# The gram directly behind the prediction on TensorE, in a delta-rule attention kernel

## The chip, the cores and the metric

One core of one Trainium2 chip. The metric is device time in microseconds of one launch; the median of several runs is given. Engines are named as in the profile: PE is TensorE (PEld its weight loads), DVE VectorE, ACT ScalarE, POOL GpSimd, SP the queue that issues all DMAs here.

## The reference

The input x has the shape (B=4, T=4096, D=512), with H=16 heads of width 32. The block is a delta-rule attention between two layer norms, then a feed-forward product with ternary weights between two more. Cut to the attention:

```python
rk = x.reshape(B, T, H, 32); rk = rk / max(norm(rk), 1e-12)      # x is the layer-normed input
wk = pad(rk[:, :-1], one step of zeros in front)                 # write key = previous read key
v, gate, beta = x @ Wv.T, sigmoid(x @ Wg.T), sigmoid(x @ Wb.T)
for t in range(T):                                               # per batch and head, S is 32x32
    pred = wk_t @ S
    S    = S + outer(wk_t, (v_t - pred) * beta_t)
    o_t  = (rk_t @ S) * gate_t
out = o @ Wo.T;  x = x + layernorm(out);  x = x + layernorm(ffn(layernorm(x)))
```

## The kernel before

The program has three stages one after the other: a setup of the weights (`setup`), the attention (`attention`) and the feed-forward product (`feed_forward`). Only PE's program in `attention` is changed.

**Tiling.** Time is cut into 128 tiles of C=32 time steps; a tile has the 4 batches x 32 steps on the 128 partitions. Within a tile the recurrence is solved in closed form: a triangular system (1 + M) e = v − pred per batch and head, with M from the gram of the keys. DVE inverts these systems by elimination, two tiles at a time, so its work in odd and in even steps of the loop differs: the matrices are turned in (L752) at the start of an even step and turned out (L816) at the end of an odd one.

**Software pipeline.** Each engine has a function `step(base, j)` that is written out for j from -13 to 134. In one step it works on many tiles at once, each shifted by a lag (`LAG_...`): tile j itself is in the chain of the state, tile j+6 (`LAG_GRAM`) has its gram made, tile j+7 (`LAG_V`) its values, keys and gates, tile j+9 (`LAG_TURN`) its x turned, tile j-3 (`LAG_Y`) its output product. An engine does its instructions in just the order in which `step` writes them; the engines meet by semaphores that count. That hand-written order is what sets the order of the work around the change.

**PE's step before** (`step`, L933 on). The names of its parts:

- `predict` (L949, 16 products on 32-column tiles of the array, 32 passes in the profile): `ps_chain` = state x `key_bd`, the block-diagonal write keys of tile j. ACT copies it to `rhs` (L611, semaphore `turned_done`).
- `turn_back` (L956, 4 transposes) turns `rhs` back into `ps_chain`; DVE then makes `rhs` = `val` − `ps_chain` (L831, semaphores `pred_psum` and `rhs_done`).
- `value(first, end)` (L925, `ps_v<-wv,xt`): some of the 12 products that make the values of tile j+7.
- gram (L981): `ps_gram` = `kt` x `kbd` for tile j+6, 16 products on 32-column tiles, copied by ACT (L674, `gram_done`) and masked by POOL (L571).
- `solve_error(half)` (L962, 32 small products): applies the inverse to `rhs`. Its wait is `error_ready`: `tt_done` and `rhs_done`.

Then x is turned (L1003, needs ACT's copy of gram, because both use the bank `ps_gram`), the keys are turned (L1011, needs ACT's copy of the values, L681, because both use `ps_v`), the output product `ps_y` and the state update (L1024) take turns, o is turned (L1048), and the gates are made (L925, `ps_v<-wgb,xt`).

**The keys for the gram.** `kbd` is block-diagonal and is filled by DMA: ACT copies the turned keys to `kt` (L702), SP waits for that copy and issues four DMAs (L456), and PE's `gram_ready` waits for them with `kbd_loaded`, in the next step:

```python
wait(pe, s["ot_done"], upto(j - 1 + LAG_OUT + 1))
wait(pe, s["xt_done"], upto(times(base, BODY, j + LAG_TURN)))
wait(pe, kbd_loaded[l % 2], halves(base, j, LAG_GRAM) * (16 * HB) + 16 * HB)
```

**SP's step** issues, in this order, the load of x (L430), two small copies of the gate (L436, L440), four DMAs of `key_bd` (L448), four of `kbd` (L456), the residual x (L461) and the store of x1 (L465).

Of the kernel before, what the change touches and what calls it, by code (L numbers as in the profile page):

```python
# [272 lines left out]
def attention(nc, io, k):  # L273
    with ExitStack() as ctx:
# [6 lines left out]
        def sem(name):  # L281
            return ctx.enter_context(nc.semaphore(name))
# [79 lines left out]
        s = {n: sem(n) for n in names}  # L362
# [7 lines left out]
        def on(base, step, lag):  # L370


            n = times(base, BODY, step + lag)
            return n, (step + lag) % BODY, not isinstance(n, int) or 0 <= n < NT

        def upto(count):
            return min(count, NT) if isinstance(count, int) else count
# [5 lines left out]
        def wait(eng, semaphore, count):  # L383

            if not isinstance(count, int) or count > 0:
                eng.wait_ge(semaphore, count)
# [497 lines left out]
        def _(pe):  # L884
# [14 lines left out]
            def error_ready(base, j):  # L899

                n, l, live = on(base, j, 0)
                if live:
                    wait(pe, s["tt_done"], times(base, BODY // 2, j // 2 + 1))
                    wait(pe, s["rhs_done"], n + 1)

            def gram_ready(base, j):

                n, l, live = on(base, j, LAG_GRAM)
                if live:
# [3 lines that stand above are left out]
# [8 lines left out]
            def project(out, lhs, weights, steps):  # L921

                for i in steps:
                    kb, (a, w) = i // 3, PARTS3[i % 3]
                    last = pe.matmul(out, lhs[:, a, kb, :], weights[:, w, kb, :], start=(i == 0), stop=(i == 3 * KB - 1))  # L925
                return last
# [4 lines left out]
            SHARE = WHOLE // 4  # L931

            def step(base, j):  # L933

                n, l, live = on(base, j, 0)
                v, v_l, v_live = on(base, j, LAG_V)
                m, m_l, m_live = on(base, j, LAG_GRAM)

                def value(first, end):
                    if v_live:  # L940
                        return project(ps_v[:, :], xt[:, v_l % 4], k["wv"], range(first, end))

                def predict():
                    if live:
                        for g in range(KB):
                            for i in range(HB):
                                h = HB * g + i
                                out = ps_chain[HD * i:HD * i + HD, P * g:P * g + P]
                                last = pe.matmul(out, state[:, l % 2, HD * h:HD * h + HD], key_bd[:, :, h, :], start=True, stop=True)  # L949
                        last.then_inc(s["turned_psum"], 1)  # L950

                def turn_back():
                    if live:
                        wait(pe, s["turned_done"], n + 1)
                        for g in range(KB):
                            last = pe.transpose(ps_chain[:, P * g:P * g + P], rhs[:, P * g:P * g + P], k["ident"][:, :])  # L956
                        last.then_inc(s["pred_psum"], 1)
# [7 lines left out]
                if live and not on(base, j - 1, LAG_Y)[2]:  # L965
                    chain_ready(base, j)
                predict()
                if v_live:
                    wait(pe, s["gexp_done"], v)
                    wait(pe, s["xt_done"], upto(v + 2))  # L970
                value(0, SHARE + 1)
                turn_back()
                value(SHARE + 1, SHARE + 2)
                gram_ready(base, j)
                value(SHARE + 2, SHARE + 3)
                if m_live:
                    for g in range(KB):
                        for b in range(B):
# [1 line left out]
                            out = ps_gram[q, :].rearrange("p (i h) -> p h i", h=H)[:, HB * g:HB * g + HB, :]  # L980
                            last = pe.matmul(out, kt[:, m_l % 2, g, q], kbd[:, m_l % 2, :, g, q], start=True, stop=True)  # L981
                    last.then_inc(s["gram_psum"], 1)
                value(SHARE + 3, 3 * SHARE - 1)
                error_ready(base, j)
                value(3 * SHARE - 1, 3 * SHARE)
                solve_error(0)
# [73 lines left out]
                if y_live:  # L1060
                    last.then_inc(s["y_psum"], 1)
            run(step)


# [293 lines left out]
```

## Time and profile before

| | us |
|---|---|
| median of 3 runs | 2329.17 |
| lowest and highest run | 2324.87, 2331.81 |
| profiled execution, span of its first to last instruction | 2313.7 |
| profiled execution, own time | not given by the page |
| PE busy | 2084.1 (90%) |
| DVE busy | 1992.1 (86%) |
| ACT busy | 1774.0 (77%) |
| POOL busy | 1729.0 (75%) |

A busy time is the sum of an engine's instructions, counted from the first start to the last end, and matmuls that overlap count once. The span does not hold what lies before the first and behind the last instruction. The attention stage runs to about 1950 us, the feed-forward stage from there to the end. A wait "PE ps_v L925 <- DMA kbd<-kt" reads: PE stood idle ahead of an instruction of line 925 that writes `ps_v`, until the DMA that writes `kbd` from `kt` had landed. Where the gram's wait stands ahead of a value product, as before the change, it is that product which shows it.

### The profile page before, as it was taken

Reading aid. Unit: us, or ns where it says so; the run is one execution under the profiler, and the core shown is the slowest. Engines: PE = TensorE matmul, PEld = TensorE weight load, DVE = VectorE, ACT = ScalarE, POOL = GpSimd, SP = SyncE. Lnnn points to the kernel's source line nnn. Section 1 sums busy time; section 2 is a strip of 40 time slices with the busy share of each in tenths; the row PEclk is TensorE's granted clock in tenths of the full one; section 3 lists DMA queues with packets and bytes.
Section 4 is the critical chain, followed back from the end, with each engine's and each line's share of the span. In section 5 each row is a group of like instructions: output and inputs, shape, how many; then the busy total and the mean of one; then the engine's idle time right before and its main releaser. Section 6 shows DMA issues by size and latency. Waiting matters only on the chain. (4 is left out here: it accounts for less than half of the span.)

```text
span 2313.7 us, 123730 instructions
## 1 busy us (share of the span) xinstructions
PE 2084.1 (90%) x50216; PEld 1316.0 (57%) x50216; DVE 1992.1 (86%) x5810; ACT 1774.0 (77%) x3756; POOL 1729.0 (75%) x3099
## 2 busy tenths in 40 slices
PE   1679999999999999999999999999999987499997
PEld 1346666666666666666655656566666654255554
DVE  5388999999999999999889999899999994588886
ACT  3667888888888888888877878788888744477775
POOL 2668888888888888888888888888888854244443
PEclk7789999999999999999999999999999988799999
DMA  2122333333333333333333333333333222488885
GB/s 86 48 65 80 98 100 98 98 98 95 99 97 99 94 94 95 95 94 94 93 91 93 94 96 91 94 97 96 100 96 99 82 78 67 150 225 229 225 231 129
DMA packets 156632, 247.69 MB, mean 107 GB/s; under 512 B 39544, under 2 KB 39552, under 8 KB 156064
## 3 DMA queue, kind: packets, MB, share of 16 engines
q1 hardware_dynamic: 156064, 239.78, 36.6%
q8 instruction: 397, 6.50, 1.2%
q14 instruction: 171, 1.40, 0.2%
HBM read 104.40 MB, written 67.11 MB: 74 GB/s over the span
## 5 line engine op out<-in xcount | busy, mean ns | idle before, releaser
L800 DVE TENSOR_TENSOR ps_elim<-ps_elim,sys 128x30 f32<-128x30 f32 (+14 forms) x1920 | 543.3, 326 | 0.7
L808 DVE TENSOR_TENSOR sys<-sys,ps_elim 128x30 f32<-128x30 f32 (+14 forms) x1920 | 534.6, 316 | 1.0
L925 PE MATMUL ps_v<-wv,xt 128*128 128x512 f16 x1536 | 435.2, 389 | 39.6 <-DVE rhs L831 16.5
L925 PE MATMUL ps_y<-wo,ot 128*128 128x512 f16 x1536 | 406.1, 386 | 17.3 <-DVE x L852 9.5
L962 PEld LDWEIGHTS ps_chain<-rhs,t_t 32*32 32x32 f32 x16384 | 257.3, 144 | 110.6 <-issue 110.5
L962 PE MATMUL ps_chain<-rhs,t_t 32*32 32x32 f32 x16384 | 286.1, 218 | 13.9 <-issue 8.5
L709 ACT ACTIVATE state<-ps_s 128x512 f32<-128x512 f32 x128 | 76.5, 598 | 265.6 <-PE ps_s L1024 263.6
L1024 PEld LDWEIGHTS ps_s<-err,key_b 32*32 32x32 f32 x16384 | 172.1, 106 | 147.4 <-issue 147.2
L1310 PE MATMUL ps_f<-wq,f_xq 128*128 128x512 f16 x1024 | 242.5, 381 | 6.8 <-DVE f_xq L1276 6.8
L538 POOL TENSOR_TENSOR x_part<-x_hat,x_part 128x512 f16<-128x512 f32 x128 | 148.7, 1162 | 131.6 <-ACT x_hat L645 111.5
L1024 PE MATMUL ps_s<-err,key_b 32*32 32x32 f32 x16384 | 205.5, 195 | 34.2 <-issue 34.2
L925 PEld LDWEIGHTS ps_v<-wv,xt 128*128 128x128 f16 x1536 | 121.0, 99 | 188.4 <-issue 120.5
L925 PEld LDWEIGHTS ps_y<-wo,ot 128*128 128x128 f16 x1536 | 130.2, 98 | 130.3 <-issue 26.3
L831 DVE TENSOR_TENSOR rhs<-val,ps_chain 128x512 f32<-128x512 f32 x128 | 87.4, 682 | 121.1 <-PE ps_chain L956 121.1
L1158 POOL TENSOR_TENSOR f_y_veps<-f_y_var,y_eps 128x1 f32<-128x1 f32 x128 | 53.6, 418 | 184.3 <-ACT f_unread L1191 183.4
L585 POOL TENSOR_TENSOR pred<-val,err 128x512 f32<-128x512 f32 x128 | 163.1, 1274 | 11.3 <-ACT err L688 11.2
L571 POOL TENSOR_TENSOR m_t<-gram,b_mask 128x512 f32<-128x512 f32 x128 | 163.5, 1277 | 5.3 <-ACT gram L674 5.2
L512 POOL TENSOR_TENSOR b_mask<-gates,neg_mask 128x512 f32<-128x512 f32 x128 | 135.5, 1059 | 32.0 <-DVE gates L879 31.9
L1310 PEld LDWEIGHTS ps_f<-wq,f_xq 128*128 128x128 f16 x1024 | 100.2, 98 | 102.0 <-DVE f_xq L1276 7.5
L577 POOL TENSOR_TENSOR o_part<-o_g,o_part 128x512 f16<-128x512 f32 x128 | 148.5, 1160 | 0.0
L949 PE MATMUL ps_chain<-key_bd,state 128*32 128x128 f32 x4096 | 139.9, 277 | 4.3 <-issue 2.8
L714 ACT ACTIVATE ot<-ps_gram 128x1024 f16<-128x1024 f16 x128 | 130.9, 1022 | 16.8 <-PE ps_gram L1048 16.7
(163 smaller groups left out, 5123.6 us busy)
## 6 DMA issues: line engine op xcount, KB each, us to landing
x_in<-in_L_attn_x SPq DMA_DIRECT2D x128, 256.0 KB
kbd<-kt SPq DMA_DIRECT2D x512, 64.0 KB, 2.1
key_bd<-key_t SPq DMA_DIRECT2D x512, 64.0 KB, 2.4
x_res<-in_L_attn_x SPq DMA_DIRECT2D x128, 256.0 KB
x_scratch<-x SPq DMA_DIRECT2D x128, 256.0 KB, 6.3
f_x<-x_scratch SPq DMA_DIRECT2D x32, 1024.0 KB, 7.6
out<-f_res SPq DMA_DIRECT2D x128, 256.0 KB, 3.9
gate<-gates SPq DMA_DIRECT2D x128, 7.9 KB
```

The source lines that it names most:

```text
L512: pool.tensor_tensor(b_mask[:, :, :], beta.unsqueeze(1).to_broadcast([P, C, H]), k["neg_mask"][:, :].unsqueeze(2).to_broadcast([P, C, H]), ...
L538: pool.tensor_tensor(x_part[:, l % 2, 1, :], x_hat[:, l % 4, :], x_part[:, l % 2, 0, :], ALU.subtract).then_inc(s["xlo_done"], 1)
L571: pool.tensor_tensor(m_t[:, :, l % 2, :], gram[:, :, :], b_mask[:, :, :], ALU.mult).then_inc(s["mt_done"], 1)
L577: pool.tensor_tensor(o_part[:, l % 2, 1, :], o_g[:, :], o_part[:, l % 2, 0, :], ALU.subtract).then_inc(s["olo_done"], 1)
L585: pool.tensor_tensor(pred[:, :], val[:, l, :], err[:, l % 2, :], ALU.subtract).then_inc(s["pred_done"], 1)
L800: dve.tensor_tensor(tmp, factors(r, c, first, end)[:, c - first:C - 1 - first, c - first:c - first + 1].to_broadcast(shape), sys[:, r, c:c ...
L808: dve.tensor_tensor(dst, dst, tmp, ALU.add).then_inc(elim_done[r], 1)
L925: last = pe.matmul(out, lhs[:, a, kb, :], weights[:, w, kb, :], start=(i == 0), stop=(i == 3 * KB - 1))
L949: last = pe.matmul(out, state[:, l % 2, HD * h:HD * h + HD], key_bd[:, :, h, :], start=True, stop=True)
L962: last = pe.matmul(ps_chain[q, e], t_t[q, l // 2 % 2, :, l % 2, h], rhs[q, e], start=True, stop=True)
L1024: last = pe.matmul(ps_s[q, e], key_b[q, l, e], err[q, l % 2, e], start=(isinstance(n, int) and n == 0 and h == 0), stop=True, skip_group_c ...
L1310: last = pe.matmul(ps_f[i][:, :], xq[:, r % 2, a, kb, P * i:P * i + P], k["wq"][:, kb, :], start=(m == 0), stop=(m == 2 * KB - 1))
```

## The change

In PE's step the gram and its `gram_ready` are moved directly behind `predict`. `turn_back` follows the gram, and the value products that stood between and around these groups (four ahead of `turn_back`, two behind it, and those behind the gram) now stand in one row behind `turn_back`, up to the one behind `error_ready`. The waits of the first value product (`gexp_done`, `xt_done`) move with it. No instruction is added or removed, and the other engines' programs are the same.

```diff
@@ -965,14 +965,7 @@
                 if live and not on(base, j - 1, LAG_Y)[2]:
                     chain_ready(base, j)
                 predict()
-                if v_live:
-                    wait(pe, s["gexp_done"], v)
-                    wait(pe, s["xt_done"], upto(v + 2))
-                value(0, SHARE + 1)
-                turn_back()
-                value(SHARE + 1, SHARE + 2)
                 gram_ready(base, j)
-                value(SHARE + 2, SHARE + 3)
                 if m_live:
                     for g in range(KB):
                         for b in range(B):
@@ -980,7 +973,11 @@
                             out = ps_gram[q, :].rearrange("p (i h) -> p h i", h=H)[:, HB * g:HB * g + HB, :]
                             last = pe.matmul(out, kt[:, m_l % 2, g, q], kbd[:, m_l % 2, :, g, q], start=True, stop=True)
                     last.then_inc(s["gram_psum"], 1)
-                value(SHARE + 3, 3 * SHARE - 1)
+                turn_back()
+                if v_live:
+                    wait(pe, s["gexp_done"], v)
+                    wait(pe, s["xt_done"], upto(v + 2))
+                value(0, 3 * SHARE - 1)
                 error_ready(base, j)
                 value(3 * SHARE - 1, 3 * SHARE)
                 solve_error(0)
```

On PE, in a step of the full pipeline, before (the names are those of the parts above; `ps_v<-wv,xt` is a value product, `ps_chain<-ident,rhs` the turn back):

```order
L949 MATMUL ps_chain<-key_bd,state 32x128 x16
L925 MATMUL ps_v<-wv,xt 128x512 x4
L956 MATMUL ps_chain<-ident,rhs 128x128 x4
L925 MATMUL ps_v<-wv,xt 128x512 x2
L981 MATMUL ps_gram<-kbd,kt 32x4x32 x16
L925 MATMUL ps_v<-wv,xt 128x512 x3
L962 MATMUL ps_chain<-rhs,t_t 32x32 x32
```

and now, at the same place:

```order
L949 MATMUL ps_chain<-key_bd,state 32x128 x16
L974 MATMUL ps_gram<-kbd,kt 32x4x32 x16
L956 MATMUL ps_chain<-ident,rhs 128x128 x4
L925 MATMUL ps_v<-wv,xt 128x512 x9
L962 MATMUL ps_chain<-rhs,t_t 32x32 x32
```

The gram has moved ahead of the turn back and of six value products; its line is now L974.

On PE, in a step ahead of the chain (tiles whose gram is made before tile 0 enters it), with the waits, before:

```order
L925 MATMUL ps_v<-wgb,xt 128x32 [waits kt_done]
L925 MATMUL ps_v<-wgb,xt 128x32 x11
L925 MATMUL ps_v<-wv,xt 128x512 [waits xt_done,gexp_done]
L925 MATMUL ps_v<-wv,xt 128x512 x4
L925 MATMUL ps_v<-wv,xt 128x512 [waits kbd_loaded0,xt_done]
L981 MATMUL ps_gram<-kbd,kt 32x4x32 x16
L925 MATMUL ps_v<-wv,xt 128x512 x6
```

and now:

```order
L925 MATMUL ps_v<-wgb,xt 128x32 [waits kt_done]
L925 MATMUL ps_v<-wgb,xt 128x32 x11
L974 MATMUL ps_gram<-kbd,kt 32x4x32 [waits kbd_loaded0,xt_done]
L974 MATMUL ps_gram<-kbd,kt 32x4x32 x15
L925 MATMUL ps_v<-wv,xt 128x512 [waits xt_done,gexp_done]
L925 MATMUL ps_v<-wv,xt 128x512 x11
```

The wait for `kbd_loaded` stood behind five value products and now stands ahead of all twelve.

## Rows read from the trace of the kernel before

**Rows 1.** Busy time by stretch: stretch, its length, each engine's busy us, clock, DMA
```profile
727.00:1299.00 572.00, 537.46 (x14823) 347.02 (x14821) 517.98 (x1660) 465.21 (x1016) 485.27 (x859) 1.00 0.33 94
1299.00:1815.00 516.00, 494.36 (x13682) 319.37 (x13680) 475.46 (x1531) 431.21 (x935) 449.13 (x794) 1.00 0.33 95
```

**Rows 2.** Waits, whole span: who waited for whom, us in total, times, longest
```profile
DVE rhs L831 <- PE ps_chain L956: 121.1, 67, 8.5
...
PE ps_v L925 <- DVE rhs L831: 16.5, 31, 1.4
...
PE ps_v L925 <- DMA kbd<-kt: 15.5, 15, 2.2
```

**Rows 3.** Timeline of PE, a middle step: start us, us, line, operation
```profile
1004.24 1.08 PE L949 MATMUL ps_chain<-key_bd,state 128*32 128x128 f32 x32
1005.25 1.04 PE L925 MATMUL ps_v<-wv,xt 128*128 128x512 f16 x4
1006.16 0.66 PE L956 MATMUL ps_chain<-ident,rhs 128*128 128x128 f32 x4
1006.65 0.59 PE L925 MATMUL ps_v<-wv,xt 128*128 128x512 f16 x2
1007.17 1.08 PE L981 MATMUL ps_gram<-kbd,kt 128*32 128x128 f32 x32
1008.19 0.82 PE L925 MATMUL ps_v<-wv,xt 128*128 128x512 f16 x3
1008.94 1.11 PE L962 MATMUL ps_chain<-rhs,t_t 32*32 32x32 f32 x64
...
1011.78 0.62 PE L1003 MATMUL ps_gram<-ident_half,x_part 128*128 128x128 f16 x8
1012.28 0.63 PE L1011 MATMUL ps_v<-ident,key 128*128 128x128 f32 x4
```

**Rows 4.** Timeline of ACT, the same step
```profile
1002.19 0.60 ACT L709 ACTIVATE state<-ps_s 128x512 f32<-128x512 f32 x1 [2.65 <-PE ps_s L1024]
...
1011.07 0.58 ACT L674 ACTIVATE gram<-ps_gram 128x512 f32<-128x512 f32 x1
1011.55 0.59 ACT L681 ACTIVATE val<-ps_v 128x512 f32<-128x512 f32 x1
...
1013.52 0.62 ACT L702 ACTIVATE kt<-ps_v 128x512 f32<-128x512 f32 x1
```

**Rows 5.** Timeline of SP: the four issues of kbd for this step
```profile
999.57 2.54 SPq L456 DMA_DIRECT2D kbd<-kt  x4
```

**Rows 6.** The tile kbd, whole span
```profile
DMA to landing us min/median/max: 1.9/2.1/3.8
```

**Rows 7.** Waits from 60 to 193 us, and PE's timeline in one such step
```profile
PE ps_v L925 <- DMA kbd<-kt: 11.4, 6, 2.2
...
72.31 1.25 PE L925 MATMUL ps_v<-wv,xt 128*128 128x512 f16 x5 [0.38 <-ACT g_exp L720]
75.58 0.58 PE L925 MATMUL ps_v<-wv,xt 128*128 128x512 f16 x1 [2.02 <-DMA kbd<-kt]
```

**Rows 8.** Waits from 193 to 515 us, and PE's timeline in one held step
```profile
PE ps_v L925 <- DMA kbd<-kt: 4.1, 9, 1.0
...
303.18 1.08 PE L949 MATMUL ps_chain<-key_bd,state 128*32 128x128 f32 x32
...
306.28 0.38 PE L925 MATMUL ps_v<-wv,xt 128*128 128x512 f16 x1 [0.31 <-DMA kbd<-kt]
...
308.72 1.11 PE L962 MATMUL ps_chain<-rhs,t_t 32*32 32x32 f32 x64
```

**Rows 9.** Timelines of SP and PE, a late step
```profile
1600.63 3.33 SPq L456 DMA_DIRECT2D kbd<-kt  x4
...
1603.79 1.08 PE L949 MATMUL ps_chain<-key_bd,state 128*32 128x128 f32 x32
...
1607.70 7.18 SPq L448 DMA_DIRECT2D key_bd<-key_t  x4
```

## The prediction

> **What bounds the kernel now.** I read busy time by stretches first, then the waits, then the timelines of PE, ACT and SP for one step of the attention stage, then the waits again by stretches. The change lies in the attention stage (to about 1950 us). From 727 to 1299 us, 39 steps of 14.7 us, PE is busy for 537 of 572 us at the full granted clock of 1.00 (2.4 GHz); from 1299 to 1815, 36 steps of 14.3 us, for 494 of 516, DVE for 475 and POOL for 449 [rows 1]. Four queues fill a step nearly whole: PE, ACT, DVE and the DMA queue of SP. So a gain on PE counts only where none of the other three ends later.
>
> The waits show which of them does. DVE waits 121.1 us for the turned-back prediction, nearly all in odd steps, and PE waits 16.5 us for DVE's `rhs` in 31 steps and 15.5 us for the block-diagonal keys `kbd` in 15 [rows 2]. These two take turns with PE; they are no slack that adds up.
>
> One step in the middle, read from PE's timeline [rows 3]: predict at 1004.24, four value products, turn back at 1006.16, two value products, gram at 1007.17, three value products, solve at 1008.94. The turned x then starts at 1011.78 and the turned keys at 1012.28. ACT in the same step [rows 4]: it begins with `state` at 1002.19 after an idle of 2.65 us, and from there it works without a gap to the copy of gram (ends 1011.65) and of the values (ends 1012.14). PE's turned x needs the first and starts 0.13 us behind it; the turned keys need the second and start 0.14 us behind it. So in such a step PE is paced by ACT's queue from predict to the keys, though it looks busy all the way.
>
> The last thing to look at is when `kbd` lands, since the gram waits for it. SP issues its four DMAs in a row after `kt` is copied. The last of the four issues of the middle step starts about 0.6 us before the row ends, at 1001.5 [rows 5], and landing takes 2.1 us in the median, 3.8 at most [rows 6]: landed at 1003.6, that is 0.6 us before predict starts.
>
> **The change, part by part.** No instruction is added or removed, on no engine. On PE the gram goes from behind the sixth value product to directly behind predict; SP's queue is as it was.
>
> (a) *Two changes of shape fall away.* The small-tile groups (predict, gram) now stand side by side. A further value product adds 0.22 us (groups of 4, 3 and 2 are 1.04, 0.82 and 0.59 long), but two of them ahead of the gram take 0.52 us and three ahead of the solve 0.75, so going over to small tiles costs about 0.09 us [rows 3]. Going back isn't shown by itself; I bound it by 0 and 0.2 (the gram's 1.02 us can't hold much more than that) and take 0.13, a little above the side that rows 3 show. With 0.04 us by which the transposes now wait for ACT behind four products, a step could save 0.26 us, over 118 steps 31 us. Of this I count nothing in the middle stretch: the turned x and keys still start when ACT's copies of gram and values end, and ACT's queue is not moved. Where DVE's `rhs` is last, it is nothing either, as DVE's own queue leads from one turn back to the next solve. It counts only as something to set against new waits.
>
> The Trainium skill, TensorEngine Tiling (Array Packing), Key Properties, says that changing the tiling mode drains TensorE; by that the order with fewer changes is the faster one, and it speaks for this change. The trace agrees: 0.09 us each time [rows 3].
>
> (b) *The gram is due 2.07 us earlier.* Before, it started 2.93 us after predict, and the product that carries its wait at about 2.6 us. Now it could start 0.9 us after predict (predict's 1.01 us less the tail that the change of shape cost). And the wait no longer has six value products in front: turn back, `rhs` on DVE and all nine products ahead of the solve are queued behind it. While `kbd` is out, PE has nothing to do. The transposes keep their time if it is landed: 0.9 + 1.02 is 1.92, what it was [rows 3].
>
> So per step the price is (landing − 0.8) where that is positive, less 0.26, less what DVE's lateness covered already. By stretches:
>
> *Start, 60 to 193 us.* In six steps without the chain PE does five products, waits for `kbd`, and does the sixth and the gram; these waits are 11.4 us in all [rows 7]. The loop kt, kbd, gram, values, keys, kt is serial there. The five products (1.25 us with their tail, five times 0.22 without) now come behind the landing: 6 x 1.08 = **6.5 us**. In three of the first four steps with the chain the keys land late as well, about 1 us each: **3 us**.
>
> *Early, 193 to 515 us, 23 steps.* PE waits for `kbd` in 9 [rows 8], although it is due only at 2.6 us. Predict starts at 303.18 and the held product at 306.28: landed near 306.2, 3.0 us after predict. Now the gram starts at 306.25, turn back 1.02 later at 307.27, then 0.49 for the transposes and 9 x 0.22 + 0.05 for the products: the solve starts at 309.8 instead of 308.72 [rows 8]. That is 1.1 us x 9 = 9.9; the other 14 land about 1 us after predict, 0.15 each, 2.1. Together **12 us**.
>
> *515 to 727 us, 15 steps.* No wait for `kbd` before. I find four steps where the four issues take as long as in rows 9 (landing about 2 us after predict), each 0.9: **3.5 us**.
>
> *Middle, 727 to 1299 us, 39 steps.* Landed before predict, as in rows 5, in nearly all of them: **0 us**.
>
> *Late, 1299 to 1815 us, 36 steps.* SP is behind. Its four issues begin at 1600.63 and last 3.33 us [rows 9], so the last starts at 1603.4 and lands at 1605.5, 1.7 us after predict (1603.79); most of the 36 are like this, 1.1 to 2.3. Before, this was early enough. Now the gram waits 0.85 us. In even steps DVE's `rhs` is late by as much and covers it. In the 18 odd ones 0.85 − 0.26 − 0.12 (the distance to ACT) = 0.45 us are left, 8 us, and up to 13 with spill into even steps. Against this, SP here issues on end (7.18 us for the four of `key_bd` just behind [rows 9]), without waiting for PE: PE held once by 0.85 us is closer to SP afterwards, and then pays only for fluctuations, 4 us. I take **6 us**.
>
> Sum: 6.5 + 3 + 12 + 3.5 + 0 + 6 = 31 us on the profiled span of 2313.7, so 2344.7. The runs' median of 2329.17 lies 15.5 us above this span (what is around it, and no time of that execution itself is given); the same 31 us on top give **2360 us**.
>
> If the cover goes: if DVE were earlier in even steps, the late stretch would pay there too; the next thing late behind a delayed turn back is `rhs`, then the value copy on ACT, then `kt`, which starts the next `kbd`. That loop is why the delay isn't made good.
>
> **The rivals.**
>
> *It gains (0.07).* If PE's own time, not ACT's, sets the step, the 0.26 us count. Against it: the 0.13 and 0.14 us by which PE follows ACT in rows 3 and 4 repeat in nearly every middle step. For it: PE's busy share. The rule of the Trainium skill's page TensorEngine Tiling points to this case too. The price: −31 us over 118 steps, +9.5 at the start, +7 early: 2315 us. It decides where ACT's copies end more than 0.12 us before PE gets there, and where `kbd` lands within 0.8 us of predict.
>
> *No difference (0.12).* If SP's queue is the real pace (each step's issues follow the last without a gap), then holding PE once brings it to SP's side, and all later waits are time that the step had to take anyway. Left are 6.5 at the start less some tenths per step in the middle: 2330 to 2336. For it: PE already waits for SP now and then. Against: in the early stretch SP begins again when `kt` is done, so a held PE holds SP.
>
> *It costs much more (0.15).* PE's small matmuls also stand idle for "issue" in the middle, where a step is 14.7 us against 14.3 in the late stretch [rows 1]. If the new phase between PE and the DMAs puts the late 36 steps into this state, that is 36 x 0.35 = 13 us, and with every landing of early and late steps unmoved relative to predict (5 + 7 more): 2329 + 31 + 25 = 2385 us, and more where both come on top of spill.
>
> **How the numbers follow.** Forecast 0.66, gain 0.07, no difference 0.12, much more 0.15. A measurement of this kernel tells about 0.3%, 7 us, from no change. The forecast and the costly case are both slower by more: 0.81. The no-difference case is taken as same, the gain as faster: 0.07. The forecast's own bounds: the early and late stretches at half (6 + 2), the start at 6.5 and a tenth gained in each of 40 middle steps (−4) give +10, 2340; the unmoved landings give 2372. To leave out no more than 2 in 10 the range goes from 2334 to 2386.
>
> **What would show it.** In the profile after: PE's timeline has 32 gram matmuls behind predict, then turn back, then nine value products. The wait for `kbd` now stands ahead of the gram, in some 50 to 60 steps instead of 15, with 40 to 60 us in total instead of 15.5, in the stretches named and hardly any from 727 to 1299. DVE's wait for the turned-back prediction grows in the same odd steps. In the middle the turned x and keys still start 0.13 us behind ACT's copies and the step keeps its 14.7 us. The solve starts about 4.4 us after predict where `kbd` is landed, 4.7 before. I am wrong if the middle steps get shorter (the gain), if few waits on `kbd` appear although PE gets no faster, or if the early stretch grows by less than 5 us.

## The result and the profile after

| | before | after |
|---|---|---|
| median | 2327.02 us (4 runs, 2323.01 to 2331.81) | 2376.68 us (4 runs, 2365.9 to 2385.66) |
| ratio, with its 95% interval | | 1.0215 [1.018, 1.025] |
| profiled execution: span | 2313.7 | 2364.2 |
| its own time | | 2365.9 |

The kernel is 49.7 us slower by the medians and 50.5 by the spans. The forecast was 2360, so the direction and the range held, and of the loss 31 us were foreseen. A second time, in a later group of runs, the changed kernel took 2350.92 against 2310.65, 1.018 [1.0159, 1.0201], 40.3 us more (a2 below).

Busy time per engine after. Against the table ahead of the prediction the busy time of all four engines is the same within 4 us; what is added is idle time:

```profile
PE 2080.2 (88%) x50216; PEld 1353.8 (57%) x50216; DVE 1988.6 (84%) x5810; ACT 1774.9 (75%) x3756; POOL 1729.9 (73%) x3099
```

PEld, the weight loads that overlap PE, is not in that table: it was 1316.0 us before and is 37.8 more now, 21.5 of it at the value products and 14.3 at the gram. e9 below has as much at the value products (21.7) but not the idle time described next, so that part at least is not its cause.

The waits of the whole span after (who waited for whom, us in total, times, longest), to be held against [rows 2]:

```profile
DVE rhs L831 <- PE ps_chain L956: 162.7, 74, 7.9
...
PE ps_gram L974 <- DMA kbd<-kt: 58.4, 44, 3.7
...
PE ps_s L1021 <- issue: 46.3, 56, 2.0
...
PE ps_chain L962 <- issue: 19.3, 29, 2.0
...
PE ps_v L925 <- DVE rhs L831: 5.5, 11, 0.9
```

PE's wait for `kbd` grew from 15.5 us in 15 steps to 58.4 in 44. DVE, which gets the turned-back prediction behind it, waits 41.6 us more, and PE hardly waits for DVE's `rhs` any longer (5.5 us, before 16.5). A second row grew that has no semaphore in it: PE idle for "issue", that is with no releaser in the profile, ahead of the state update (34.2 us in 41 before) and of the solve (8.5 in 11 before).

PE's timeline, a middle step after (start us, us, line, operation), the counterpart of [rows 3]:

```profile
1033.40 1.08 PE L949 MATMUL ps_chain<-key_bd,state 128*32 128x128 f32 x32
1034.30 1.06 PE L974 MATMUL ps_gram<-kbd,kt 128*32 128x128 f32 x32
1035.33 0.66 PE L956 MATMUL ps_chain<-ident,rhs 128*128 128x128 f32 x4
1035.82 2.11 PE L925 MATMUL ps_v<-wv,xt 128*128 128x512 f16 x9
1037.85 1.11 PE L962 MATMUL ps_chain<-rhs,t_t 32*32 32x32 f32 x64
...
1040.87 0.62 PE L1000 MATMUL ps_gram<-ident_half,x_part 128*128 128x128 f16 x8
1041.45 0.63 PE L1008 MATMUL ps_v<-ident,key 128*128 128x128 f32 x4
```

and ACT's in that step, the counterpart of [rows 4]:

```profile
1040.24 0.58 ACT L674 ACTIVATE gram<-ps_gram 128x512 f32<-128x512 f32 x1
1040.71 0.59 ACT L681 ACTIVATE val<-ps_v 128x512 f32<-128x512 f32 x1
```

This is the order as built. The gram starts 0.90 us behind predict, and the solve 4.45 us (4.70 in [rows 3]), so the two saved changes of shape are there (over the 39 middle steps the median distance to the solve is 4.57 us, before 4.70). They bring nothing here: the turned x starts at 1040.87, 0.05 us after ACT's copy of gram ends, the turned keys 0.15 us after the copy of the values.

The Trainium skill, TensorEngine Tiling (Array Packing), Key Properties, says that changing the mode drains TensorE. The trace agrees in kind: with two changes fewer the solve comes 0.25 us nearer to predict in this step, and 0.13 us in the median of the middle steps. No run shows that it pays here.

A held step in the early stretch: PE's timeline,

```profile
402.12 1.08 PE L949 MATMUL ps_chain<-key_bd,state 128*32 128x128 f32 x32
405.88 1.93 PE L974 MATMUL ps_gram<-kbd,kt 128*32 128x128 f32 x32 [2.69 <-DMA kbd<-kt]
407.75 1.12 PE L956 MATMUL ps_chain<-ident,rhs 128*128 128x128 f32 x4
408.65 2.31 PE L925 MATMUL ps_v<-wv,xt 128*128 128x512 f16 x9
```

SP's issues of `kbd` for it,

```profile
399.00 3.58 SPq L456 DMA_DIRECT2D kbd<-kt  x4
```

and the same microseconds by window (stretch, its length, busy us of PE, PEld, DVE, ACT, POOL, granted clock, DMA share, GB/s):

```profile
402.10:405.60 3.50, 1.10 (x33) 0.81 (x32) 3.39 (x10) 3.50 (x10) 3.34 (x7) 1.00 0.50 112
405.60:409.10 3.50, 3.22 (x38) 2.53 (x39) 1.50 (x5) 3.47 (x9) 2.90 (x7) 0.51 0.25 95
409.10:416.00 6.90, 6.90 (x219) 4.59 (x217) 6.86 (x24) 3.17 (x6) 5.23 (x10) 1.00 0.28 80
```

Two things are to be seen. The last of the four issues started at 401.98 and its DMA landed 3.8 us later; the median from an issue's start to landing is 2.0. PE could go on only at 405.88. And behind PE's idle of 2.69 us the granted clock is 0.51, the 1.2 GHz level, for one stretch: gram to turn back takes 1.87 us where it takes 1.03 at full clock. The prediction had no term for this.

The Trainium skill, TensorE: Matmul & The Clock Gate, HAM oscillation — how this bites in real kernels, tells of a kernel in which waits for a DMA let the clock fall, so that the next burst starts at half rate. The trace agrees in kind, 1.00 before the idle and 0.51 behind it.

Where the time went, by PE's `predict` of the tiles that bound each stretch (one profiled execution of each kernel, us; the kernels are named below). The short form of the orders: P predict, G gram, T turn back, V with a number so many value products. A number of a tile is that of the tile whose `predict` begins there; the stretches begin at the `predict` of tiles 4, 27, 42, 81 and 117.

| kernel | start to tile 4 | 4 to 27 | 27 to 42 | 42 to 81 | 81 to 117 | rest |
|---|---|---|---|---|---|---|
| before (P V4 T V2 G V3) | 193.2 | 320.6 | 213.7 | 571.7 | 516.0 | 498.5 |
| before again, b2 | 187.1 | 324.4 | 213.7 | 570.7 | 518.1 | 502.5 |
| after (P G T V9) | 201.7 | 339.1 | 215.5 | 575.1 | 535.6 | 497.2 |
| after again, a2 | 201.7 | 330.9 | 214.5 | 574.6 | 532.1 | 496.8 |
| e1, wait early only | 203.6 | 329.1 | 219.1 | 575.7 | 518.4 | 502.0 |
| e9 (P V1 G T V8) | 203.2 | 334.3 | 216.9 | 573.2 | 522.3 | 497.5 |
| e8 (new order ahead of the chain only) | 200.4 | 326.8 | 215.6 | 571.1 | 518.3 | 501.1 |
| e5 (P V4 G T V5) | 194.2 | 332.0 | 218.6 | 581.0 | 525.8 | 501.8 |
| e2, after without the wait | 176.1 | 325.3 | 212.4 | 572.2 | 527.6 | 498.2 |
| e3, before without the wait | 181.5 | 324.9 | 214.0 | 568.7 | 518.8 | 501.2 |
| e4 (P V4 T V4 G V1) | 181.7 | 322.2 | 212.6 | 572.7 | 516.7 | 499.5 |

The two executions of the kernel before differ by 6 us in the first stretch and by 0 to 4 in the others; smaller differences between rows carry nothing.

The last stretch took the most: 19.6 us of the 50.5. PE's waits there before, 1299 to 1815 us:

```profile
PE ps_v L925 <- DVE rhs L831: 9.7, 15, 1.4
PE ps_s L1024 <- issue: 5.1, 6, 1.1
PE ps_y L925 <- DMA key_bd<-key_t: 4.7, 10, 1.1
PE ps_chain L962 <- issue: 1.8, 3, 0.9
```

and after, 1331 to 1867 us:

```profile
PE ps_s L1021 <- issue: 16.9, 21, 1.5
PE ps_chain L962 <- issue: 9.4, 18, 1.2
PE ps_gram L974 <- DMA kbd<-kt: 8.0, 14, 1.7
PE ps_y L925 <- DMA key_bd<-key_t: 1.3, 1, 1.3
PE ps_v L925 <- DVE rhs L831: 0.3, 1, 0.3
```

The wait for `kbd` is 8.0 us and took the place of the wait for `rhs`, 9.7. What came on top is idle for "issue", from 6.9 to 26.3 us.

Idle time of this kind is not new: in the stretch from tile 42 to 81 every kernel here has 29 to 41 us of it (before 32.9, after 37.0), most of it ahead of the state update. Split at tile 97, the last stretch shows that in the changed kernel this state of the middle goes on for some 16 tiles more (us; in brackets the idle for "issue" ahead of the solve, the state update and the turns):

| kernel | 81 to 97 | 97 to 117 |
|---|---|---|
| before | 233.4 (6.9) | 282.5 (0.0) |
| before again, b2 | 232.9 (5.0) | 285.2 (0.3) |
| after | 239.2 (17.4) | 296.4 (9.0) |
| after again, a2 | 240.1 (17.1) | 292.1 (7.7) |
| e1, wait early only | 232.4 (2.7) | 286.0 (0.0) |
| e9 (P V1 G T V8) | 230.4 (2.9) | 291.9 (5.9) |
| e2, after without the wait | 240.3 (20.2) | 287.4 (0.0) |
| e3, before without the wait | 231.4 (4.6) | 287.4 (0.0) |

### The profile page after: what moved, and what is told of

It is laid out like the page before. It is cut to its first block and busy times, and to the rows that moved or that the text cites. A ratio compares the mean times of both kernels' runs of the same rounds, so it can differ in the third digit from the quotient of the medians.

```text
span 2364.2 us, 123730 instructions
## 1 busy us (share of the span) xinstructions
PE 2080.2 (88%) x50216; PEld 1353.8 (57%) x50216; DVE 1988.6 (84%) x5810; ACT 1774.9 (75%) x3756; POOL 1729.9 (73%) x3099
## 5 line engine op out<-in xcount | busy, mean ns | idle before, releaser
L925 PE MATMUL ps_v<-wv,xt 128*128 128x512 f16 x1536 | 388.7, 387 | 11.1 <-DVE rhs L831 5.5
L962 PE MATMUL ps_chain<-rhs,t_t 32*32 32x32 f32 x16384 | 293.5, 218 | 25.9 <-issue 19.3
L925 PEld LDWEIGHTS ps_v<-wv,xt 128*128 128x128 f16 x1536 | 142.5, 100 | 163.2 <-issue 39.3
L974 PE MATMUL ps_gram<-kbd,kt 128*32 128x128 f32 x4096 | 149.5, 289 | 58.8 <-DMA kbd<-kt 58.4
L974 PEld LDWEIGHTS ps_gram<-kbd,kt 128*32 128x32 f32 x4096 | 121.2, 116 | 71.8 <-issue 71.3
```

Of the source, the lines that this page charges most:

```text
L962: last = pe.matmul(ps_chain[q, e], t_t[q, l // 2 % 2, :, l % 2, h], rhs[q, e], start=True, stop=True)
```

## The experiments

Two theories stood after this. **W**: the early wait for `kbd` makes the loss, with all that is queued behind it. **O**: a part comes from the order itself, from predict and gram side by side, apart from any wait.

The runs were timed in three groups beside the kernel before, each on its own chip: e1 to e4 (before 2323.6), a2 and e5 to e7 (2310.65), b2 and e8 to e10 (2322.35). Totals of different groups are compared by their ratios.

**e1, the wait alone.** The order stays that of before; only the wait moves to where the change has it.

```diff
                 predict()
+                gram_ready(base, j)
...
-                value(SHARE + 1, SHARE + 2)
-                gram_ready(base, j)
-                value(SHARE + 2, SHARE + 3)
+                value(SHARE + 1, SHARE + 3)
```

> The order of before, with the gram's waits (kbd landed among them) placed directly behind predict; the gram itself, the turn back and the value products stay where they were. Theory W (the cost is that the wait for kbd is due 1.7 us earlier and holds all that is queued behind it): 2365 to 2385 us, as the change or a little more, since no change of shape is saved. Rival S (the new order itself, or the phase between PE and the DMAs that it sets, costs): within 10 us of before, 2317 to 2337.

Measured: 2350.54 against 2323.6, 1.0127 [1.0085, 1.0169], 27 us. So the wait alone makes more than half of the 40 to 50. That it doesn't make all is shown against the first interval of the change, from 1.018 on, and not against a2's, which begins at 1.0159. In its trace the wait has another name, since it stands ahead of the first value product and another semaphore than `kbd` is inferred; PE in a step of the last stretch:

```profile
1428.80 1.08 PE L949 MATMUL ps_chain<-key_bd,state 128*32 128x128 f32 x32
1430.55 1.02 PE L925 MATMUL ps_v<-wv,xt 128*128 128x512 f16 x4 [0.67 <-issue]
```

The last stretch, where the changed kernel lost 16 to 20 us, is only 2.4 longer than before (518.4). What the wait costs lies at the start and in the stretches up to tile 42. And it isn't that PE didn't wait late: idle for "issue" ahead of `ps_v` is 23.0 us in 31 steps there (before none), and that is most likely this wait. It took the place of others: `rhs` is down from 9.7 to 1.8 us.

**e2 and e3, both orders without the wait.** Gram reads a constant in place of `kbd` (e2 in the order after, e3 in that of before), and the wait for the DMA is put off to the turned keys. The edit to the gram is the same in both:

```diff
-                            last = pe.matmul(out, kt[:, m_l % 2, g, q], kbd[:, m_l % 2, :, g, q], start=True, stop=True)
+                            last = pe.matmul(out, kt[:, m_l % 2, g, q], k["ident"][:, :].rearrange("p (i t) -> p i t", t=C), start=True, stop=True)
```

> The changed order, but the gram reads a constant tile (the identity) in place of kbd, so that it never waits; the same DMAs of kbd are issued, and PE waits for them only ahead of turning the keys. Left out: the block-diagonal keys in the gram. Theory W: the whole loss is gone, 2305 to 2330 us, no more than 5 us above the same cut in the order of before. Rival S: 15 to 30 us above that one, with steps of 15 us after 1340 us and idle time of the small products for issue as in the change.

> The same cut in the order of before. Theory W: it loses the 15.5 us of waits for kbd, of which about half were on the path: 2312 to 2327 us. The gain theory of the prediction (PE's own time sets the step, two changes of shape saved are worth up to 31 us): the changed order with this cut is 15 to 30 us below this run. Theory that ACT paces the step: less than 6 us below.

Measured: e2 2314.0, 0.9964 [0.9947, 0.998]; e3 2310.86, 0.9949 [0.9929, 0.9969]. Without the wait the two orders are 3 us apart, and their intervals overlap. The saved changes of shape gain nothing in the total, and W looks complete. But the last stretch speaks against it: 527.6 us in e2, 518.8 in e3. PE's waits of e2 there, 1286 to 1813 us, with no `kbd` in the program's way:

```profile
PE ps_s L1022 <- issue: 15.2, 16, 1.5
PE ps_y L924 <- DMA key_bd<-key_t: 7.6, 12, 1.0
PE ps_v L924 <- DVE rhs L831: 7.1, 8, 1.8
PE ps_chain L961 <- issue: 4.9, 9, 1.0
```

20.1 us of idle for "issue", against 4.6 in e3. That is O, without any wait. All of it lies before tile 97: there e2 has no other wait on PE, and takes 8.9 us more than e3; behind it the two take the same 287.4. At the start e2 is 5 us shorter than e3 (176.1 and 181.5; no more than two runs of one kernel differ there), and so the total hides it.

**e4, the other way.** If an early gram waits, a late one shouldn't: gram directly ahead of the solve, its wait one product ahead.

```diff
                 turn_back()
-                value(SHARE + 1, SHARE + 2)
+                value(SHARE + 1, 3 * SHARE - 1)
                 gram_ready(base, j)
-                value(SHARE + 2, SHARE + 3)
+                value(3 * SHARE - 1, 3 * SHARE)
...
-                value(SHARE + 3, 3 * SHARE - 1)
                 error_ready(base, j)
-                value(3 * SHARE - 1, 3 * SHARE)
```

> The gram the other way: directly ahead of the solve, with the wait for kbd one value product ahead of it, behind eight. The wait is due 1 us later than before, and one change of shape is saved. Theory W: the early waits for kbd vanish and those of the start shrink by 3 x 0.22 us in six steps, the rest as before: 2310 to 2325 us. Rival: the gram's copy on ACT comes late and holds the turned x: 2330 to 2345.

Measured: 2310.71, 0.9939 [0.9916, 0.9962]. It is faster than both kernels, and as fast as e3, which has no wait for `kbd` ahead of the gram at all. Its waits, whole span:

```profile
PE ps_chain L962 <- DVE rhs L831: 22.2, 31, 2.0
PE ps_v L925 <- DMA kbd<-kt: 12.9, 17, 1.4
```

12.9 us for `kbd` are left, 2.6 less than in [rows 2], and to tile 4 it needs 181.7 us, as e3 does.

**a2, the change once more**, with no edit and in another group of runs, to see how firm the 50 us are.

> The changed kernel once more, for the spread of its runs and a second profile. Its four runs so far lie between 2366 and 2386 us. Theory F (beside the wait, the new order leaves more idle time for issue in PE's small products from 1340 us on): again 15 us or more of such idle time above before in that stretch. Rival R (that stretch was an accident of the one profile): little of it, and the median nearer to the run with only the wait moved, 2350 to 2360. Theory C (the clock): again a handful of steps between 200 and 1900 us in which turn back starts 1.8 us behind the gram and not 1.0, behind waits for kbd of 2 us and more.

Measured: 2350.92, 1.018 [1.0159, 1.0201], 40.3 us. The wait for `kbd` was 48.3 us in 38 steps. The early stretch gave 10.3 us where the first profile gave 18.5; the last one 16.1 and 19.6.

**e5, gram behind four products.** Predict and gram are apart again, with turn back behind the gram. Against the kernel before:

```diff
                 value(0, SHARE + 1)
-                turn_back()
-                value(SHARE + 1, SHARE + 2)
                 gram_ready(base, j)
-                value(SHARE + 2, SHARE + 3)
...
-                value(SHARE + 3, 3 * SHARE - 1)
+                turn_back()
+                value(SHARE + 1, 3 * SHARE - 1)
```

> Predict, four value products, gram, turn back, five value products: the wait for kbd is due 0.9 us later than in the change (1.8 us after predict) but still ahead of the turn back, and predict and gram are apart. Theory W: most late landings of the late stretch (1.1 to 1.8 us) fall inside, so 2330 to 2350 us. Theory F, if it is the many small products of predict and gram in one row that run PE out of instructions: the idle time for issue falls back to that of before. Rival: 2360 and more, as the turn back is now 0.9 us later in every step and DVE's loop is the pace.

Measured: 2352.11, 1.0182 [1.0166, 1.0198], as slow as the changed kernel, but in other rows. Waits, whole span:

```profile
DVE rhs L831 <- PE ps_chain L956: 187.5, 68, 8.7
PE ps_v L925 <- DVE rhs L831: 41.4, 46, 1.8
...
PE ps_s L1022 <- issue: 25.6, 32, 2.3
PE ps_gram L978 <- DMA kbd<-kt: 23.8, 19, 2.6
```

`kbd` is down to 23.8 us and the idle for "issue" ahead of the state update is below that of before (34.2), but turn back comes a gram later than before and PE now waits 41.4 us for DVE's `rhs` (16.5 before). So this order doesn't single out O: it has a bound of its own, the loop turn back, `rhs`, solve.

**e9, one product between.** The smallest step away from the change: `kbd` is needed 0.3 us later. The waits of the first value product (`gexp_done`, `xt_done`) come ahead of the gram with it; everything else is as after. Against the kernel before:

```diff
-                value(0, SHARE + 1)
-                turn_back()
-                value(SHARE + 1, SHARE + 2)
+                value(0, 1)
                 gram_ready(base, j)
-                value(SHARE + 2, SHARE + 3)
...
-                value(SHARE + 3, 3 * SHARE - 1)
+                turn_back()
+                value(1, 3 * SHARE - 1)
```

> The change with one of the nine value products put between predict and gram. The wait for kbd is due 0.3 us later. Theory F as 'predict and gram side by side are more small products in a row than PE is fed with': idle time for issue falls by 10 us or more and the time to about 25 to 32 us above before. Rival (it is the lateness of all that follows, not the adjacency): idle time and time stay within 6 us of the change.

Measured: 2350.81, 1.011 [1.0089, 1.013], 28.5 us over before by the medians and 25.5 by the ratio, in the range of e1 and clear of a2's interval. `kbd` waits are 45.9 us in 42 steps, nearly those of a2. PE in the last stretch, 1327 to 1850 us:

```profile
PE ps_gram L978 <- DMA kbd<-kt: 7.8, 18, 1.0
PE ps_v L925 <- DVE rhs L831: 7.6, 11, 1.2
PE ps_chain L962 <- issue: 4.8, 9, 0.9
PE ps_s L1022 <- issue: 4.1, 6, 0.9
```

The wait for `kbd` is as in the changed kernel (8.0), the idle for "issue" is 8.9 us instead of 26.3, and the stretch 522.3 us instead of 535.6. One product of 0.3 us between the two groups of small matmuls takes back 13 us here (10 against a2), 9 to 10 of it before tile 97, and of the whole 12 to 21 us by the medians (40.3 and 49.7 less 28.5) or 0.7 to 1.05% by the ratios. That is O, beside the wait.

**e8, the start alone.** The new order only in steps ahead of the chain; in the others the order of before.

```diff
+                if live:
+                    predict()
...
+                else:
+                    predict()
+                    gram_ready(base, j)
...
+                    turn_back()
...
+                    value(0, 3 * SHARE - 1)
```

> The changed order only in the steps ahead of the chain (six grams), the order of before from tile 0 on. Theory W with the prediction's term: 6.5 us at the start and nothing later, so 4 to 8 us above before. Rival: the later phases move with the start (which step meets which DMA), and it is 10 us and more off in either direction.

Measured: 2327.91, 1.0022 [1.0003, 1.0041], 5.6 us by the medians and 5.1 by the ratio, with an interval from 0.7 to 9.5 us. The prediction's term was 6.5, which agrees, as half of it would. Its last stretch (518.3 us) is that of before, so the new order at the start alone doesn't bring the idle time there.

**b2, the kernel before once more**, beside e8 to e10.

> The kernel before once more, for a second profile against which the stretches of the other runs can be set: ratio 1.00, waits for kbd in about 15 steps, idle time of PE for issue within 10 us of the first profile's 61, of it 15 us or less from step 81 to step 117.

Measured: 2324.64 against 2322.35, 1.001 [0.9995, 1.0025]. Its profile gives the second row of the table.

**e6 and e7, `kbd` issued by ACT.** To take SP's queue out of it, ACT issues the four DMAs directly behind the copy to `kt`, in the order of before (e6) and of after (e7); SP no longer does.

```diff
                                          ACT.Copy).then_inc(s["kt_done"], 1)
...
+                    wait(act, s["kt_done"], n + 1)
+                    for i in range(HB):
+                        act.dma_start(kbd[HD * i:HD * i + HD, l % 2, i, :, :],
+                                     kt[HD * i:HD * i + HD, l % 2, :, :]).then_inc(kbd_loaded[l % 2], 16)
```

> The order of before, the four DMAs of kbd issued from ACT's queue directly behind its copy of kt, so that SP has 2.5 us less to issue per step and the keys land about 4 us after kt, 0.4 us after predict. Theory W: waits for kbd only ahead of the chain; a little faster than before, 2300 to 2322 us. Rival: ACT's idle 2.65 us behind kt is eaten by the issues and the state copy comes late: 2330 and more.

> The changed order with the DMAs of kbd on ACT's queue. Theory W: with the keys landed by 0.5 us after predict the new order costs only its 4 us at the start and the issue time of theory F: 5 to 20 us above the same edit in the order of before. If the loss were the order alone, it stays at 40 us and more above that run.

Measured: e6 2398.61, 1.0394 [1.0361, 1.0428]; e7 2408.91, 1.0424 [1.0407, 1.044]. The issues themselves eat ACT. The waits of e6, whole span:

```profile
ACT state L707 <- issue: 214.1, 65, 4.0
```

The copy of `state`, which stands behind the issues, comes late by up to 4.0 us, and that is on the chain. The two differ by 10 us with intervals that overlap, and e7 still waits 40.9 us for `kbd`; this pair can't decide on W. It does bear on O: in the last stretch the idle for "issue" ahead of the solve and the state update is 22.3 us in e7, where the groups touch, and 3.9 in e6.

**e10, on top of e4.** ACT's square for the norm of x moves behind the copy to `kt`, so that its copies of gram and values come earlier. The prediction held that ACT paces PE in the middle.

```diff
-                    wait(act, s["ss_sum"], n - 1)
-                    nc.scalar.activation(x_sq[:, l % 2, :], x_in[:, l % 4, :], ACT.Square,
...
                                          ACT.Copy).then_inc(s["kt_done"], 1)
...
+                    wait(act, s["ss_sum"], n - 1)
+                    nc.scalar.activation(x_sq[:, l % 2, :], x_in[:, l % 4, :], ACT.Square,
```

> The gram directly ahead of the solve (as in e4_gram_late), and ACT's third pass over the normed x (the squares, 0.8 us) moved from ahead of gram and value copies to behind the copy of kt, where ACT stood idle for 2.65 us. If ACT's queue paces PE up to the turned keys, as the prediction says, the turned keys start 0.6 to 0.7 us earlier after predict in the middle steps, and the whole is 5 to 25 us below e4_gram_late's 0.994 of before. If PE's issue or DVE takes it up at once: the same time as e4_gram_late.

Measured: 2311.21, 0.9924 [0.9892, 0.9955], the time of e4. In the median of the middle steps ACT's copy of gram starts 6.13 us behind predict (6.84 in e4), but the turned x and keys start 7.43 and 7.96 us behind it (7.47 and 8.05 in e4), and the stretch from 42 to 81 takes 572.8 us, as in e4. The expectation was wrong: PE itself is close behind ACT's pace, and taking ACT away buys 0.04 to 0.09 us at that place.

## Why the prediction was right, and where it was short

**Direction and mechanism: right.** The wait for `kbd` stands where it was said to and in the stretches named: 25.6 us to 200 us, 20.5 from 200 to 530, and 0.4 us in two steps from 750 to 1340. It came in 44 steps (50 to 60 were forecast) with 58.4 us (40 to 60). That the total fits doesn't confirm its parts: in the late stretch far fewer steps waited than forecast (below). DVE's wait grew with it. e1 shows that this wait costs 27 us by itself, e2 and e3 that nothing is left of the loss in total without it.

**(a) The saved changes of shape: right.** They are in the timeline and are worth nothing in total: e2 isn't faster than e3. That refutes the rival of a gain.

**(b) by stretches**, added us of the two profiles of the changed kernel against the profiled before:

| stretch | forecast | first profile | a2 |
|---|---|---|---|
| start and first chain steps | 6.5 + 3 | 8.5 | 8.5 |
| early | 12 | 18.5 | 10.3 |
| 515 to 727 | 3.5 | 1.8 | 0.8 |
| middle | 0 | 3.4 | 2.9 |
| late | 6 | 19.6 | 16.1 |

Against the second profile of before, b2, the first stretch is 14.6 us in both, early 14.7 and 6.5, and late 17.5 and 14.0; the others change by 1 us or less. So the terms can be told to some 6 us at the start and 4 us elsewhere.

*Start*: right within that. e8 gives 5.1 (0.7 to 9.5) for the 6.5.

*Early*: the term "1.1 us x 9" was mis-sized in one profile and about right in the other. `kbd` held PE in 15 steps rather than 9, 20.5 us in all. And behind four of these waits the clock fell, as shown at 405.88. Each such gram takes 1.72 to 1.94 us instead of 1.08, and turn back and products behind it lose as much again; by the distance from gram to the solve it is 1.5 to 1.6 us each, some 6 us. With them off, 18.5 is 12.5. In a2 the waits are 12.4 us, and the clock fell twice in this stretch.

*Middle*: "0 us" was right within some 4 us. The step was said to keep 14.7 us; it is 14.75 (575.1 / 39). The reason given, that ACT's queue paces PE, is only half of it: e10 relieved ACT by 0.7 us and the step stayed the same. What sets its length in the middle wasn't found.

*Late*: this is the term that failed, in two ways. "Now the gram waits 0.85 us", in most of the 36 steps, would be some 30 us of waits. It was 8.0 us in 14 steps (a2: 6.1 in 12). With the order of before and the wait alone moved, e1, PE does wait about so, 23.0 us in 31 steps, but that costs 2.4 us in this stretch, less than the 6. What was missing is the other part: predict and gram side by side leave PE idle for "issue" further on, at the solve and the state update, 26.3 us against 6.9. It needs the two groups to touch (8.9 in e9, 4.2 in e5) and it needs no wait (20.1 in e2, 4.6 in e3), though the stretch grows by 9 us without the wait and by 14 to 20 with it. The rival "it costs much more" had named just this: a new phase that puts the late steps into the state of the middle, for 13 us. It came true for part of them. In e2 the state lasts to tile 97, 16 steps of 15.0 us instead of 14.5, and costs 8.9 us. It came in all four kernels whose groups touch in the late steps (after, a2, e2, e7) and in none of the other ten, so it is a cost of the new order itself, on top of the forecast's terms, and not a case in place of them.

*Slips in the sum*: by [rows 3] the gram comes 2.03 us earlier (2.93 less 0.9), not 2.07, and half of the late term is 3, not 2. The first enters no term, the second moves the lower bound by 1 us.

**The start of the sum: right by luck.** The 15.5 us between the profiled span and the median were put down to what lies around the span. In all other kernels here the own time is only 1.7 us above the span: this execution was a quick one. Adding to the median was right all the same, but not for the reason given. The spans (50.5) and the medians (49.7) agree because the profiled execution after was a quick one too, 10.8 us below its median.

**No difference, with SP's queue as the pace**: refuted, e1 is slower by 1.27%.

**What stays open.** Why PE stands idle for "issue" when the two groups touch: the records show no releaser, and no run here looks at how PE is fed. Also open is how the wait and the order together make more in the late stretch (14 to 20) than each by itself (2.4 and 9). What comes on top lies behind tile 97: 292.1 and 296.4 us there with both, 282.5 to 287.4 in before, b2, e1, e2 and e3. e9, with the wait and one product between, has 291.9, so it isn't the touching that makes this part.

**The version to keep** is e4, gram late: 0.9939 [0.9916, 0.9962], 12.9 us below before by the medians. Its first stretch is 5 to 12 us shorter than in the two profiles of before, and half or more of the gain lies there. e10 isn't told apart from it.

## What to carry to other kernels

A wait belongs to the place in the queue, not only to the instruction that needs it: moving a waiting step forward past work that could have run puts all of that work behind the transfer. Ask of every group that depends on a DMA how late it may stand; here the same gram, placed ahead of its next consumer, turned a loss of 2% into a gain of 0.6%. Price an order by measuring it with and without the wait, and with one product more between the groups: totals hid an effect of 9 us that the stretches showed, and a cut at the right tile showed that it was an old state lasting longer.

## What wasn't expected of the hardware

**The clock falls inside a busy kernel.** PE's grams behind waits for `kbd` in the changed kernel, some of the early stretch and one of the late:

```profile
422.89 1.94 PE L974 MATMUL ps_gram<-kbd,kt 128*32 128x128 f32 x32 [2.15 <-DMA kbd<-kt]
...
468.22 1.08 PE L974 MATMUL ps_gram<-kbd,kt 128*32 128x128 f32 x32 [2.34 <-DMA kbd<-kt]
497.52 1.72 PE L974 MATMUL ps_gram<-kbd,kt 128*32 128x128 f32 x32 [2.26 <-DMA kbd<-kt]
...
1648.05 1.93 PE L974 MATMUL ps_gram<-kbd,kt 128*32 128x128 f32 x32 [0.63 <-DMA kbd<-kt]
```

An idle of 2.15 us made the next gram run at the low level, one of 2.34 us did not. At 1648.05 the idle of 0.63 followed one of 1.26 us for `key_bd`, with one product and a predict between. In the kernel before no stretch between 158 and 1877 us is at the low level. But it doesn't take a wait for `kbd`. In e3, which has none ahead of its gram, the clock falls behind an idle of 1.19 us for `rhs`; it is 1.00 on both sides of the stretch shown (a row of PE's timeline, then the same microseconds by window):

```profile
1453.96 0.38 PE L924 MATMUL ps_v<-wv,xt 128*128 128x512 f16 x1 [1.19 <-DVE rhs L831]
...
1455.50:1458.90 3.40, 3.40 (x78) 2.46 (x77) 3.37 (x13) 1.58 (x5) 3.07 (x8) 0.51 0.31 90
```

So a wait of 2 us can cost 3.5, and from its length alone one can't say whether it will.

**A landing isn't a constant.** From the start of the last issue to landing it was 3.8 us in the held step shown; over all issues of `kbd` in the changed kernel it is 1.9 us at least, 2.0 in the median and 4.0 at most.

**PE stands idle with no semaphore behind it** in every kernel here from tile 42 to 81, 29 to 41 us. Where predict and gram touch, this goes on to tile 97, and one ordinary product between them ends it: the 36 late steps are 10 to 13 us shorter in e9 than in the two profiles of the changed kernel. The reason stays open.
